# Two token-sorting stages of a macaron transformer block, with their last block of 512 tokens worked as two parts of 256

## The reference

```python
x = x + 0.5 * L0_ffn(layernorm(x))      # 32 experts of 64, sigmoid gates, top 4 of 32
x = x + L0_attn(layernorm(x))           # linear attention, 16 heads of 8, 32 features
x = x + 0.5 * L0_ffn(layernorm(x))      # as the first, same weights
x = x + 0.5 * L1_ffn(layernorm(x))      # 8 experts of 512, top 2 of 8 with capacity 2048, gelu
x = x + L1_attn(x)                      # 16 heads of 64: softmax weights of a token for itself
x = x + 0.5 * L1_ffn(layernorm(x))      # as above, same weights
```

```python
idx1, idx2 = top two of logits = xt @ Wg
pos = cumsum(mask) - mask               # place in the expert's queue
xe[idx, pos] += xt * keep               # rows sorted by expert
ye = gelu(xe @ W1 + b1) @ W2 + b2       # per expert
out = ye[idx1, pos1] * w1 + ye[idx2, pos2] * w2
```

## Time and profile before

| | before |
|---|---|
| median of the runs | 1663.5 us |
| the profiled execution | 1655.25 us |
| its span | 1653.5 us |
| TensorE busy | 84% |
| VectorE busy | 82% |
| ScalarE busy | 63% |
| GpSimd busy | 52% |
| mean granted TensorE clock | 0.947 |

### The profile page before, as it was taken

One profiled execution on the slowest core, in us unless ns is written; L12 is line 12 of the kernel. 1 busy time (PEld: TensorE's weight loads), 2 busy tenths in 40 slices (PEclk: granted clock), 3 DMA queues, 4 the chain that ended last, 5 costly groups with the idle time before them and its releaser, 6 DMA issues.

```text
span 1653.5 us, 28336 instructions
## 1 busy us (share of the span) xinstructions
PE 1396.0 (84%) x8249; PEld 1065.6 (64%) x8249; DVE 1349.5 (82%) x3897; ACT 1037.4 (63%) x2298; POOL 855.1 (52%) x745
## 2 busy tenths in 40 slices
PE   5999998898999994999458888878888799859991
PEld 4777877655666663999446566555565566549991
DVE  7699999567767676888789999999999767868887
ACT  7544542364223234999569989999989832349991
POOL 5856653210134333577656656666656315637762
PEclk9999999998999997999779999999999899969996
DMA  9991001000111104222399700000000001112225
GB/s 194 180 181 28 1 21 33 2 1 1 29 33 44 32 19 96 61 75 75 87 192 181 126 2 1 1 1 2 1 1 1 1 7 38 41 52 75 72 67 152
DMA packets 156499, 91.26 MB, mean 55 GB/s; under 512 B 19413, under 2 KB 151206, under 8 KB 156352
## 3 DMA queue, kind: packets, MB, share of 16 engines
q1 hardware_dynamic: 142464, 70.52, 23.1%
q0 software_dynamic: 9664, 16.89, 3.2%
q10 hardware_dynamic: 4224, 2.10, 0.4%
HBM read 31.93 MB, written 60.53 MB: 56 GB/s over the span
## 4 chain that ended last, share of the span: by engine, by line
PE 50%; DVE 13%; POOL 11%; issue 11%; ACT 11%; DMA 3%; POOLq 0%; SPq 0%; DVEq 0%; ACTq 0%
PE psum L1374 10%; PE psum L2815 8%; POOL answers L2431 8%; ACT psum L2915 7%; PE psum L661 5%; PE psum L662 4%; PE psum L663 4%; DVE psum L2935 4%; PE psum L2794 2%; PE psum L2795 2%; PE psum L2796 2%; PE psum L1129 1%; PE psum L1131 1%; PE psum L1130 1%; DVE x L2557 1%
## 5 line engine op out<-in xcount | busy, mean ns | idle before, releaser
L2935 DVE CUSTOM_DVE_ANT_0 psum<-psum,cmask 128x128 f32<-128x128 f32 (+7 forms) x512 | 375.2, 786 | 24.8 <-PE psum L2815 24.5
L2915 ACT ACTIVATE psum<-psum,gate 128x128 f32<-128x128 f32 (+7 forms) x512 | 367.0, 719 | 41.9 <-DVE gate L2935 34.8
L1374 PE MATMUL psum<-raw_all,w 128*128 128x512 f32 x384 | 195.4, 592 | 1.5 <-DVE raw_all L1515 1.5
L661 PE MATMUL psum<-xl,wreg 128*128 128x512 f32 x320 | 181.1, 566 | 2.6 <-ACT psum L2915 1.3
L1513 DVE SCALAR_TENSOR_TENSOR raw_all<-psum,hg 128x512 f32<-128x512 f32 x128 | 88.1, 690 | 57.7 <-PE psum L663 56.4
L2815 PE MATMUL psum<-spare_sets_room 64*128 64x384 f32 (+3 forms) x768 | 93.4, 375 | 42.0 <-ACT psum L2915 42.0
L2815 PE MATMUL psum<-hh,hl 64*128 64x384 f32 (+3 forms) x768 | 91.8, 371 | 42.3 <-ACT psum L2915 42.3
L662 PE MATMUL psum<-xh,wreg 128*128 128x512 f32 x320 | 126.6, 396 | 0.0
L663 PE MATMUL psum<-xh,wreg 128*128 128x512 f32 x320 | 126.5, 395 | 0.0
L2431 POOL DMA_INDIRECT answers<-ed,xl x90 | 100.3, 1114 | 31.1 <-issue 30.5
L2815 PEld LDWEIGHTS psum<-spare_sets_room 64*128 64x128 f32 x768 | 71.0, 193 | 66.3 <-ACT psum L2915 54.7
(11 more groups left out here) (437 smaller groups left out, 4211.1 us busy)
## 6 DMA issues: line engine op xcount, KB each, us to landing
rows<-blank SPq DMA_DIRECT2D x146, 258.0 KB, 7.5
xl<-rows SPq DMA_DIRECT2D x58, 193.5 KB
raw_all<-answers SPq DMA_DIRECT2D x32, 256.0 KB, 4.2
w<-in_L_ffn_W_dram SPq DMA_DIRECT2D x16, 256.0 KB, 3.1
x<-in_L_attn_x_dram SPq DMA_DIRECT2D x4, 512.0 KB, 5.8
out_dram<-x ACTq DMA_DIRECT2D x8, 256.0 KB, 4.3
answers<-ed,xl POOLq DMA_INDIRECT x90, 2.4
answers<-row,xl POOLq DMA_INDIRECT x84, 2.5
```

The source lines that it names most:

```text
L661: pe.matmul(dst, wh, xl[:, blk(i)], start=start, stop=False)
L1374: pe.matmul(bank(B_OUT[i % 2]), col(dn, j), hidden[:, n % HID, :], start=(j == 0), stop=(j == nf - 1)).then_inc(S["dn_done"], 1)
L2915: return act.activation(src, src, ACT.Exp, bias=kept_at(arg, u, q, a), scale=-1.0, accum_out=kept_at(esum, u, q, a))
L2935: return dve.tensor_tensor_reduce(src, src, mask, 1.0, 3e38, ALU.add, ALU.min, kept_at(arg, u, q, a))
```

## The change

The eight blocks become nine parts: seven of four tiles and two of two. In both stages the last block is worked as two parts, each with its own nf steps (all up and down products with 256 columns in place of 512), its own chain and its own sends (four and four in place of eight). Waits that counted blocks now count parts, and the two row buffers change places (even parts use `row`, odd ones `row_even`), so that the last part sends from `row`, as the last block did. `paced` keeps its rule, with the end at 9 nf up products in place of 8 nf. The gates of the last block are still set, spread and copied once.

```diff
+PARTS = [(i * BT, BT) for i in range(NB - 1)] + [(NT - BT, BT // 2), (NT - BT // 2, BT // 2)]
+NPARTS = len(PARTS)
...
+    def tiles_of(k):
+        at, n = PARTS[k]
+        return bass.ds(at, n)
+
+    def columns_of(k):
+        at, n = PARTS[k]
+        return bass.ds(at * P, n * P)
+
+    def sent_by(a, k):
+
+        return 16 * 2 * sum(PARTS[m][1] for m in range(a, k, 2))
...
     def row_of(i):
-        return row[:] if i % 2 else row_even
+        return row_even if i % 2 else row[:]
...
-        pool.wait_ge(S["filled"], BT * (i + 1))
+        pool.wait_ge(S["filled"], sum(PARTS[i]))
         pool.wait_ge(S["tagged"], i + 1)
         apart(pool, spare_p).then_inc(S["spaced"], 1)
-        for t in range(BT):
+        for t in range(PARTS[i][1]):
...
             if n == "v":
-                wait_sent(sp, S, NB)
+                sp.wait_ge(S["sent"][1], sent_by(1, NPARTS))
...
-        PERIODS = NB + 1 + LAST_PLACE // nf
+        PERIODS = NPARTS + 1 + LAST_PLACE // nf
...
+        def width(i):
+            return PARTS[i][1] * P
+
+        def gates_now(i):
+
+            at = PARTS[i][0] % BT * P
+            return hg[:, 1 - min(i, NB - 1) % 2, at:at + width(i)]
...
-                product3(pe, bank(B_UP[n % len(B_UP)]), col(up[0], j), col(up[1], j), i).then_inc(S["up_done"], 1)
+                product3(pe, bank(B_UP[n % len(B_UP)])[:, 0:width(i)], col(up[0], j), col(up[1], j), columns_of(i)
+                         ).then_inc(S["up_done"], 1)
...
-                pe.matmul(bank(B_OUT[i % 2]), col(dn, j), hidden[:, n % HID, :], start=(j == 0), stop=(j == nf - 1)
+                pe.matmul(bank(B_OUT[i % 2])[:, 0:width(i)], col(dn, j), hidden[:, n % HID, 0:width(i)], start=(j == 0), stop=(j == nf - 1)
                           ).then_inc(S["dn_done"], 1)
...
                 for j in range(nf):
-                    if i < NB:
+                    if i < NPARTS:
                         up_product(i, j)
...
             def paced(k, m):
-                return min(nf * (k + 1) + PLACE + 2 + m * nf // 8, NB * nf)
+                return min(nf * (k + 1) + PLACE + 2 + m * nf // 8, NPARTS * nf)
...
-                sp.wait_ge(S["dn_done"], NB * nf)
+                sp.wait_ge(S["dn_done"], NPARTS * nf)
                 heads_load(sp, H, S)
```

More of the change, by code:

```diff
@@ L657, in build, with product3 @@
     FILL = -1.0
[L659 to L663, removed]
+    def product3(pe, dst, wh, wl, some, start=True, stop=True):
+        pe.matmul(dst, wh, xl[:, some], start=start, stop=False)
+        pe.matmul(dst, wl, xh[:, some], start=False, stop=False)
+        return pe.matmul(dst, wh, xh[:, some], start=False, stop=stop)
     def wait_past(e, semaphore, count):
@@ L727, in choose_step @@
     def choose_step(dve, i, k, S, found):
-        four = blk(i, BT)
+        some, nt = tiles_of(i), PARTS[i][1]
+        half = E1 * nt
         if k < COUNT_AT:
@@ L740, in choose_step @@
         if k == CHOOSE - 2 and i >= 2:
[L741 removed]
+            dve.wait_ge(S["sent"][i % 2], sent_by(i % 2, i))
         def wide(v):
[L744 to L749, removed]
@@ L750, in choose_step @@
-        before_e, behind_e = (run[:].rearrange("p (e k) -> p e k", e=E1 + 1)[:, a:a + E1, 0] for a in range(2))
+            return v.unsqueeze(2).to_broadcast([P, nt, E1])
+        raw = found[:, RAW_AT:RAW_AT + nt * E1].rearrange("p (t e) -> p t e", t=nt)
+        below = L[:, some, :]
+        back8 = iota8[:].unsqueeze(1).to_broadcast([P, nt, E1])
+        m1, m2 = (m16[:, c * E1:(c + 1) * E1, some].rearrange("p e t -> p t e") for c in range(2))
+        run_now, place_now = run[:, 0:(E1 + 1) * 2 * nt], place_flat[:, 0:2 * half]
@@ L751, in choose_step @@
+        before_e, behind_e = (run_now.rearrange("p (e k) -> p e k", e=E1 + 1)[:, a:a + E1, 0] for a in range(2))
+        by_expert = place_now.rearrange("p (e k) -> p e k", e=E1)
+        eq_now, rest_now, most_now, top_now = eq[:, 0:nt], rest[:, 0:nt], most[:, 0:nt], top_at[:, 0:nt]
+        sums_now = row_sum[:, :, 0:nt]
         if k == 0:
-            last = dve.tensor_reduce(most[:], raw, AX.X, ALU.max)
+            last = dve.tensor_reduce(most_now, raw, AX.X, ALU.max)
         elif k == 1:
-            last = dve.tensor_tensor(below, raw, wide(most), ALU.subtract)
+            last = dve.tensor_tensor(below, raw, wide(most_now), ALU.subtract)
@@ L761, in choose_step @@
         elif k == 5:
-            last = dve.scalar_tensor_tensor(rest[:], m1, -3e38, below, ALU.mult, ALU.add)
+            last = dve.scalar_tensor_tensor(rest_now, m1, -3e38, below, ALU.mult, ALU.add)
         elif k == 6:
-            last = dve.tensor_reduce(most[:], rest[:], AX.X, ALU.max)
+            last = dve.tensor_reduce(most_now, rest_now, AX.X, ALU.max)
         elif k == 7:
-            last = dve.tensor_tensor(eq[:], rest[:], wide(most), ALU.is_equal)
+            last = dve.tensor_tensor(eq_now, rest_now, wide(most_now), ALU.is_equal)
@@ L1387, in turn_x @@
                 pe.wait_ge(S["added"], k + 1)
-                for t in range(BT):
-                    last = pe.transpose(tiles(B_TURN)[:, t, :], x[:, k * BT + t, :], ident[:])
+                for t in range(PARTS[k][1]):
+                    last = pe.transpose(tiles(B_TURN)[:, t, :], x[:, PARTS[k][0] + t, :], ident[:])
                 last.then_inc(S["xT_done"], 1)
@@ L2422, in gpsimd @@
         def gpsimd(pool):
-            pool.wait_ge(before["spaced"], NB + (before["heads"] is not None))
+            pool.wait_ge(before["spaced"], NPARTS + (before["heads"] is not None))
             for b in range(SPARSE):
```

119 lines of the change are left out of this document (61 added, 58 removed).

## The result

The changed kernel took 1675.31 us in the median of its runs (1668.33 to 1678.79), the kernel before beside it 1663.62: a ratio of 1.007, 95% interval 1.0051 to 1.0089, so 8.5 to 14.8 us slower. The forecast was 1668.5 us, with a range to 1674.

A forecast was written before the change was run, and what follows sets the result against it. TensorE paces stage 1's last period, then a chain through o decides; GpSimd's sends close stage 2. Stage 1 +4.65 (6.35 - 1.7) and stage 2 +0.4 give +5.05 on a median of 1663.5: 1668.5 us, range 1662.5 to 1674.

The forecast's parts named there:

- Narrow step 0.79 us: TensorE, both stages: a 256-column step takes 0.79 us, so two cost 1.58 where one full step cost 1.56.
- Waits at the fixed step: Stage 1: TensorE waits for the chain at the count, 2.8 us in part 7's period and 1.6 in part 8's.
- The period of part 8: Stage 1, narrow steps with the two-tile chain of part 7: 16.3 us, including waits of 1.6 and 0.2.
- The period of part 7: Stage 1, narrow steps with the chain of full block 6: 18.7 us, including 3.3 us of waits.
- The sum above has 0.5 us for this: Stage 1: VectorE's two-input picks slowed beside GpSimd's low parts; 0.5 us in the sum, 0.85 by the page.
- the clock: Rival: TensorE's clock falls to 1.2 GHz in stage 1's narrow periods; +4 us, total +9; chance 0.17.
- Behind the last down product: End of stage 1: loads of v and o follow q and k at once, so this chain gains 1.7 us.
- Stage 1 in all: Stage 1's sum: last down product 6.35 us later, less 1.7 gained behind it, +4.65 us.
- Stage 2, forecast +0.4: Stage 2: GpSimd's sends decide; the last is issued near 1460.9 in place of 1460.46, +0.4 us.
- Stage 2's tail decides by its chain: Rival: part 8's row numbers come after GpSimd is free; stage 2 costs +4, total about +9; chance 0.10.
- The third, not slower: Rival: VectorE's chain and PSUM banks cover TensorE's waits in stage 1; total -2 to +1 us; chance 0.13.
- signs of being wrong: Idle before counts under 0.5 us; clock under 1.00; sends, not o, before next_low; GpSimd idle before part 8's sends.

The follow-up runs named there:

- quiet session: Session measuring the changed kernel, unaltered, whose trace has no stall; there were two, at +5.1 and +8.5 us against the kernel before.
- no_low_part: Changed kernel with GpSimd's low part of expert 7's weights replaced by zero fills; 1664.53 us, +4.7 against the kernel before.
- filled_wait: Changed kernel with 14 unread 512-column products on TensorE in stage 1's wait before the count; 1666.28 us, +6.2 against the kernel before.
- after: The profiled execution of the changed kernel's first measurement, 1678.79 us; the median of those runs was 1675.31 us.
- four controls: The changed kernel again, unaltered: three measured +5.1, +14.0 and +8.5 us against the kernel before, one a single execution of 1669.49 us.
- stalled traces: Two traces of the changed kernel, unaltered, with stalls in stage 2; their measurements were +11.7 and +14.0 us against the kernel before.
- control_2: The changed kernel again, unaltered, as one single profiled execution; 1669.49 us, 9.6 above the median of the kernel before.
- only_stage1_b: Last block in two parts in stage 1 alone, stage 2 whole, measured a second time; 1668.62 us, +9.8 against the kernel before.

## Why the prediction was wrong

The direction was right, and so was the kind of mechanism: a chain of fixed length met at a fixed step. The forecast of +5.0 lies near the +5.1 of one quiet session and 3.5 below the +8.5 of the other. That nearness is luck: it comes of two errors of opposite sign, 4.5 us too little in stage 1 and 2.4 too much in stage 2. The measurement on record lay 1.3 us above the range. Stage 1 by itself does not carry it there: with both stages as the quiet traces have them, +7.4, the time would be 1671 and inside the range. The rest of the measured +11.7, some 4 us, stays without a shown cause; the stalls in stage 2 cost 5.0 in its trace (58.8 against 53.8).

**Narrow step 0.79 us:** right (616.74 to 617.53). **Waits at the fixed step:** right in kind. The count of part 7's period waited 3.8 us (forecast 2.8), the one of part 8's 1.43 (1.6). In part 7's period the picks were there 14.3 us after its start (611.02 - 596.69, forecast 12.4) and TensorE 10.5 us after it (forecast 9.6), so the two differences hide each other in part. The period of part 8 took 16.6 us (16.3).

**The period of part 7**, 18.7 us, is the step that failed: it took 22.6. Of the 3.9 us too much, 3.4 are busy time (18.83 against 15.4) and 0.5 idle time (3.8 against 3.3). Two terms were too small. "The sum above has 0.5 us for this", on picks beside GpSimd's low parts: it was 1.7, by no_low_part. The bound stood in the row that I used: L774's 1.02 against 0.17 is 0.85 for one instruction, and two picks with two SBUF inputs fell into GpSimd's 2.5 us (1.28 + 1.26), each held until GpSimd's instruction ended. By the Trainium skill (GPSIMD Engine Reference, Key points) GpSimd and VectorE share their SBUF interfaces and two-input instructions contend; the runs agree, since fills without an input left the picks at 0.19 and 0.30, and even the 0.85 that I had named as the price by the page was half of it. The second is the clock. I had it as a rival at 0.17 and in the sum at nothing. It fell behind the longer wait (0.51 over 5.62 us) and cost 1.9 us by filled_wait, in only one of the two narrow periods: behind the wait of 1.43 us the clock stayed at 1.00. By the Trainium skill (TensorE: Matmul & The Clock Gate, HAM oscillation), as weighed in the prediction, waits between bursts can bring the clock down; the trace agrees in the first period (granted 0.51) and not in the second (1.00). With both taken away, "down" is +6.8 against the forecast's +6.35, by one trace.

**Behind the last down product** I forecast a gain of 1.7 by v and o following q and k at once. v was issued 5.2 us behind the last down product (641.17 - 635.95; before, 7.3), not at once, and k took 7.5 us to land instead of 6.6. ScalarE was the line, as forecast, and the deal ended at +14.8 (forecast +14.2, before +15.9). The gain was 1.3 in after (26.8 us from "down" to "low" against 28.1), and 0.3 to 1.1 in the four controls. Stage 1 in all: **+9.2 in after, forecast +4.65**; +8.7 to +10.3 in the six other traces with the same stage 1.

**Stage 2, forecast +0.4:** -2.0 in quiet sessions. I took the start of the period 3.3 us too late (count 5 at 1425.30 stands at the end of its second step, not ahead of it), and let GpSimd's line of sends begin at a fixed time; its head moves with the up products that pace it. That the chain does not decide was right in the quiet sessions, but by nothing to spare, for both arrive at 1464.4. In the two stalled traces the gain is lost, and stage 2 costs 3.0 and 5.7 us.

**Rivals.** The clock was a second term and no rival, as both happened at once. "Stage 2's tail decides by its chain" did not happen in quiet sessions; in the stalled traces it did, but because of the stalls and not of longer periods. The third, not slower, fell with the first wait. Two of the signs of being wrong that the prediction names came true in after: a clock under 1.00 in a narrow period (0.85 in that of part 7) and an idle GpSimd before part 8's sends.

## What to carry to other kernels

Work in smaller parts helps the resource whose queue closes a stage (here a line of sends, 2 us) and hurts where a chain of fixed latency is met at a fixed step: the products shrink, the chain does not. Ask of each stage which of the two closes it, and cut only there. The gain ends where the chain arrives as late as the queue. Where a wait is forecast to grow, put the contention of what newly runs beside it and the clock behind it into the sum and not among the rivals, for they come with the wait.

## What the runs showed of the hardware

A VectorE pick of 128x32 with two SBUF inputs took 1.07 and 1.14 us beside GpSimd's two-input subtractions of 128x512, and 0.30 and 0.19 beside GpSimd's fills of the same size. A reduction with one input took 0.19 there as elsewhere.

After a wait of 3.8 us TensorE ran at its lower level for 5.6 us. After a wait of 2.1 us (no_low_part) it was there too, with a granted clock of 0.50 from 613.00 to 615.00. After a wait of 1.4 us it was not, nor with matmuls that nobody reads in the long wait. In control_2 and only_stage1_b, same program in that stretch, "down" came 1.2 us earlier than in the other controls, and in control_2 the steps from 615.75 on are faster again, after three behind the count and not four: the length of the slow stretch is not fixed.

In two of five traces of the changed kernel TensorE and VectorE, and in part ScalarE, stood still at about the same time for 2 to 4 us in stage 2, while GpSimd went on sending (1465.66, 1466.92 and 1468.18 in after). This was not traced to a cause.
